# A two-layer model on one core: attention that scores once and transposes in fp32, and a quarter of the scan's input products made on GpSimd

## The reference

```python
x = _layernorm(x + mamba_block(x))      # two selective scans (forward, backward), then a small FFN
x = _layernorm(x + gated_mlp(x))        # silu(x W1) * (x W2), two gelu layers of 512, W3
x = _layernorm(x + attention(x))        # below
x = _layernorm(x + experts(x))          # 8 experts, top 2 by a gate
```

```python
dA = jnp.exp(dt_t[:, :, None] * A)
h = dA * h + (dt_t * u_t)[:, :, None] * B_t[:, None, :]
y = jnp.einsum('bds,bs->bd', h, C_t)
```

```python
scores = jnp.einsum('bqhrd,bkhd->bhrqk', q, k) * scale
scores = jnp.where(causal, scores, jnp.finfo(scores.dtype).min)
probs = jax.nn.softmax(scores, axis=-1)
y = jnp.einsum('bhrqk,bkhd->bqhrd', probs, v)
```

## Time and profile before

| | |
|---|---|
| median of 3 runs | 1955.34 us (1953.61 to 1958.84) |
| profiled execution, its own time | 1948.13 us |
| its span in the trace | 1946.3 us |
| mean granted clock of TensorE | 0.932 of full speed |
| PE busy | 1654.4 us, 85% of the span |
| DVE busy | 1541.2 us, 79% |
| ACT busy | 1114.8 us, 57% |
| POOL busy | 752.7 us, 39% |
| DMA | 309.48 MB, mean 159 GB/s |

### The profile page before, as it was taken

How to read it: one execution, slowest core, us unless ns; L and a number is a source line. 1 busy time by engine, 2 the same in 40 slices (tenths; PEclk the granted TensorE clock), 3 DMA queues, 4 the chain that set the end, 5 groups by cost and what they waited for, 6 DMA issues and landing times.

```text
span 1946.3 us, 26951 instructions
## 1 busy us (share of the span) xinstructions
PE 1654.4 (85%) x8352; PEld 768.0 (39%) x8352; DVE 1541.2 (79%) x2163; ACT 1114.8 (57%) x1553; POOL 752.7 (39%) x601
## 2 busy tenths in 40 slices
PE   3533588889988999889988999889988999889888
PEld 2200134344444435334444435344444435344545
DVE  3999799779995999779995999779996999631514
ACT  3544486467854885567853885567754884433132
POOL 0455454334632454334632454334533454410102
PEclk7655699999999999999999999999999999989999
DMA  7999998667864896668864796667864896500000
GB/s 187 230 244 248 220 242 203 153 156 199 204 153 121 188 216 163 165 143 196 200 156 118 184 218 163 168 147 198 194 156 112 195 219 165 120 0 0 6 1 6
DMA packets 107915, 309.48 MB, mean 159 GB/s; under 512 B 15970, under 2 KB 32244, under 8 KB 107764
## 3 DMA queue, kind: packets, MB, share of 16 engines
q1 hardware_dynamic: 93556, 279.32, 60.9%
q10 hardware_dynamic: 14208, 28.32, 4.5%
HBM read 287.67 MB, written 19.92 MB: 158 GB/s over the span
## 4 chain that ended last, share of the span: by engine, by line
PE 36%; DVE 28%; issue 13%; ACT 13%; DMA 4%; SPq 2%; ACTq 2%; DVEq 1%; POOL 0%; POOLq 0%
PE ps_pair L716 12%; DVE sb_hst L1295 10%; PE ps_pair L813 7%; DMA sb_ring<-spread_dram 4%; PE ps_pair L872 4%; PE ps_pair L801 4%; DVE ps_in L1287 3%; PE ps_pair L892 3%; ACT sb_mix L1129 3%; DVE sb_nmax L1436 2%; ACT sb_ring L971 2%; ACT L940 2%; DVE sb_u L1339 2%; PE ps_pair L816 1%; DVE sb_eh L1504 1%
## 5 line engine op out<-in xcount | busy, mean ns | idle before, releaser
L1567 POOL TENSOR_TENSOR sb_hc<-sb_hst,sb_crep 128x512 f32<-128x512 f32 x512 | 652.8, 1284 | 916.2 <-DVE sb_hst L1295 642.0
L1295 DVE TENSOR_TENSOR_SCAN sb_hst<-sb_ring,ps_in 128x512 f32<-128x512 f32 x512 | 620.0, 1211 | 5.0 <-ACT sb_ring L971 2.5
L971 ACT ACTIVATE sb_ring<-sb_ring,sb_A 128x512 f32<-128x512 f32 x512 | 344.8, 713 | 207.6 <-DMA sb_ring<-spread_dram 116.9
L1287 DVE TENSOR_TENSOR ps_in<-sb_ring,ps_brow 128x512 f32<-128x512 f32 x512 | 354.4, 692 | 29.5 <-DMA sb_ring<-spread_dram 11.5
L940 ACT ACT_TABLE_LOAD x181 | 232.2, 1283 | 46.4 <-issue 39.4
L872 PE MATMUL ps_pair<-sb_mix,sb_ew 128*128 128x512 f32 x512 | 250.0, 624 | 4.6 <-ACT sb_ea L1163 2.2
L651 PE MATMUL ps_y<-sb_hc,sb_const 128*32 128x512 f32 x1024 | 154.2, 678 | 98.8 <-POOL sb_hc L1567 68.7
L813 PE MATMUL ps_pair<-sb_g,sb_h 128*128 128x512 f32 x320 | 168.6, 652 | 15.8 <-DVE sb_dd L1275 5.1
L801 PE MATMUL ps_pair<-sb_h,sb_g 128*128 128x512 f32 (+3 forms) x512 | 165.0, 452 | 13.1 <-DVE sb_nmax L1436 7.8
L872 PEld LDWEIGHTS ps_pair<-sb_mix,sb_ew 128*128 128x128 f32 x512 | 96.6, 198 | 139.1 <-issue 95.3
L892 PEld LDWEIGHTS ps_pair<-sb_ew,sb_eh 128*128 128x128 f32 x1024 | 121.6, 192 | 26.2 <-issue 17.8
(11 more groups left out here) (219 smaller groups left out, 2065.0 us busy)
## 6 DMA issues: line engine op xcount, KB each, us to landing
sb_ring<-spread_dram SPq DMA_DIRECT2D x512, 512.0 KB, 5.9
spread_dram<-sb_dd ACTq DMA_DIRECT2D x32, 512.0 KB, 3.7
sb_brep<-cut_dram ACTq DMA_DIRECT2D x16, 256.0 KB, 4.1
...
```

Source lines behind the costliest of these rows:

```text
L971: act.activation(ring[:, n % RING, 0, :], ring[:, n % RING, 0, :], ACT.Exp, scale=A[d][:, g:g + 1]).then_inc(sem["dA"], 1)
L1287: dve.tensor_tensor(ps_in[n % 2][:], ring[:, n % RING, 1, :], ps_brow[:], ALU.mult).then_inc(sem["dbu"], 1)
L1295: dve.tensor_tensor_scan(hst[:, HST_SLOT[n], :], ring[:, n % RING, 0, :], ps_in[n % 2][:], 0.0, ALU.mult, ALU.add).then_inc(sem["scan"], 1)
L1567: pool.tensor_tensor(hc[:, n % 6, :], hst[:, HST_SLOT[n], :], crep[n // NU][:], ALU.mult).then_inc(sem["hc"], 1)
```

## The change

**Attention.** Scores are made once, with queries on the partitions. A score step is now one bank for one key/value group k, one tile t of 128 queries, and as many of its four heads as fit: four for t = 0, two for t = 1, one for t = 2 and 3 (22 steps, `SCORES`). DVE takes the maximum from the bank (`nmax`), ACT the exponential from the same bank with the negated maximum as bias and with the sum of each row as a second output (`zsum`), one instruction for each head (32). PE transposes the exponentials back in fp32, four blocks of 128x128 for each of 20 `turn` steps; ACT copies the bank into `pT`, and `values` multiplies it with the latent values. The reciprocals of the sums (DVE) are spread over the rows by a product with the identity (`zs`), which ACT copies into `rz` for DVE's `yT`. The second score products, the split, the products with `pick` and `ones`, and 1/sum by exp(-ln) are gone. A sequence's attention has 46 `r` steps in place of 28. Banks are now handed out singly, least recently used first, and `att0` and `att1` hold one each.

**Scans.** Of each four units the last (n % 4 == 3, `POOLED`) has its product with B's rows made by POOL, in place in `ring`, from a copy of B's rows in SBUF (`brep`, now one for each direction). DVE skips `drive` for it, and its `scan` reads both inputs from `ring` in SBUF. These are 16 of a sequence's 64 units.

**Orders.** All strings are new. In DVE's, 88 of its 128 `u` steps stood ahead of the first attention step, with 37 inside the attention; now they are 99 and 25.

```diff
@@ constants and tables
-TILES = ((0, 3), (1, 2))
-ROUNDS = rounds()
+POOLED = [n % 4 == 3 for n in range(UNITS)]
+GROUPS = [(k, t) for k in range(KV) for t in (range(TT) if k == 0 else reversed(range(TT)))]
+SCORES = [(k, t, heads) for k, t in GROUPS for heads in {0: [range(REP)], 1: [range(0, 2), range(2, REP)]}.get(t, [[r] for r in range(REP)])]
+TURNS_P = [(k, t, j) for k, t in GROUPS for j in range(t + 1)]
+PSLOT, PTSLOT = 7, 3
...
 ORDER = dict(
     DVE=(
-        "uxuuxxxurxuxxguuuuuuuuxuxuururxuuxuhrxuuxruuuuuuuuuhrruhuuruhuxuuxruuururuuuuxuuhgruruuuuuuruuuxuuhhuuruuxuuur"
+        "uxuxxxxuuuuguuxuuruuxuuxxuuuruuuuurrhuuuruuxuhuuruuruuruhuururruuururxurhxruguuuuuuhuuuuuurhuuruuuuhuuuuuuuxgu"
...
@@ TensorE
+                def scores(u):
+                    k, t, heads = SCORES[u]
...
+                    for n, r in enumerate(heads):
+                        pe.matmul(o[:, n * w:(n + 1) * w], qT[:, tl, r, :], kz[:, 2 * k + hf, 0:w], start=True, stop=False)
+                        ins = pe.matmul(o[:, n * w + t * P:(n + 1) * w], identb[:], maskb[:], start=False, stop=True)
                     done(ins)
...
+                def turn(x):
+                    k, t, j = TURNS_P[x]
+                    o = claim(f"t{x}")
+                    pe.wait_ge(sem["pexp"], row("pexp", group_scores(k, t)))
+                    for r in range(REP):
+                        slot, at_r = slot_of(k, t, r)
+                        ins = pe.transpose(o[:, r * P:(r + 1) * P], pexp[slot][:, at_r + j * P:at_r + (j + 1) * P], ident)
                     done(ins)
...
+                    elif what == "z":
+                        values(LAST_TURN[i])
+                        o = claim(f"zs{i}")
+                        pe.wait_ge(sem["zr"], row("zr", i + 1))
@@ ScalarE
-                        act.activation(pexp[i % 3], ps_pair[0][:], ACT.Exp).then_inc(sem["pexp"], 1)
...
+                        for n, r in enumerate(heads):
+                            ins = act.activation(pexp[i % PSLOT][:, n * w:(n + 1) * w], bank[tab[f"s{i}"][0][0]][:, n * w:(n + 1) * w], ACT.Exp,
+                                                 bias=nmax[:, k, t, r:r + 1], accum_out=zsum[:, k, t, r:r + 1])
+                        ins.then_inc(sem["pexp"], 1)
+                    elif what == "t":
...
+                        act.activation(pT[:, i % PTSLOT, :], full(f"t{i}")[:], ACT.Copy).then_inc(sem["pt"], 1)
@@ VectorE
+                if POOLED[n]:
+                    return
                 dve.wait_ge(sem["scan"], row("scan", n - 1))
...
             def scan(row, n):
-                dve.wait_ge(sem["dbu"], row("dbu", n + 1))
+                if POOLED[n]:
+                    dve.wait_ge(sem["pbu"], row("pbu", sum(POOLED[:n]) + 1))
+                    dbu = ring[:, n % RING, 1, :]
...
@@ GpSimd
+            def drive(row, n):
+                if n % NU <= 3:
+                    pool.wait_ge(sem["brep"], row("brep", 16 * (n // NU + 1)))
+                pool.wait_ge(sem[f"ring{n % RING}"], row(f"ring{n % RING}", 16 * (n // RING + 1)))
+                pool.tensor_tensor(ring[:, n % RING, 1, :], ring[:, n % RING, 1, :], brep[n // NU][:], ALU.mult
+                                   ).then_inc(sem["pbu"], 1)
+
             def units(at, prev):
                 for n in range(UNITS):
+                    if n + 1 < UNITS and POOLED[n + 1]:
+                        drive(at(0), n + 1)
```

278 lines of the change are left out of this document (123 added, 155 removed).

## The result

The changed kernel takes 1980.4 us (median of 4 runs, 1978.4 to 1982.8); the kernel before takes 1955.4 beside it. The ratio is 1.0126, with a 95% interval of 1.0105 to 1.0147: slower by 25 us, where I had forecast 1865 us, and outside my range. The profiled execution has a span of 1981.0 us and a mean granted clock of 0.908; before it was 1946.3 and 0.932.

A forecast was written before the change was run, and what follows sets the result against it. Passes were taken as bound by DVE outside the attention and by PE in its second half. Five passes -60, second and last sequences -20, flush -15, first sequence +2: -93 from 1948.1, plus 7.2, gives 1862, stated as 1865 us (1825 to 1905).

The forecast's parts named there:

- 56 + 150.5 = 206.5: One pass of the loop: attention plus the stretch outside it, forecast 206.5 us, 12 us less than before.
- The attention at 56: Attention of a pass: engines' work of 44, 41 and 45 us plus a quarter for hand-overs, 56 us (bounds 46 and 78).
- -16 us of about 50: PE's work in each attention: second scores and smaller products go, 80 fp32 transposes come, -16 us of about 50.
- stalls at `yT`: DVE's idle time before `yT` in the attention: forecast to shrink from 15.6 us to about 8 a pass.
- Outside at 150.5: Stretch of a pass outside the attention, bound by DVE: forecast to grow from 140.4 to about 150.5 us.
- The moved units: DVE outside the attention: 11 half units moved there, 5.5 scans and 5.5 products, +10.5 us a pass.
- -8.3 of products: DVE outside the attention: twelve of the products given to POOL lie there and save 8.3 us a pass.
- +6.5 of locks: DVE outside the attention: pooled scans with two SBUF inputs wait for POOL, +6.5 us a pass.
- The third: Rival, chance 0.09: score banks held until ACT is done make PE stand; attention 75 us, pass +7, program 2005 us.
- its 68 us: Attention length in a pass beyond which the bank waits would decide: 56 + 12 = 68 us.
- The second: Rival, chance 0.12: ACT bounds the attention (sums 0.3 each) or PE's clock falls; pass +6 us, program 1915 us.
- The first: Rival, chance 0.12: every pooled scan waits for a full POOL operation; 8 us more a pass, program 1929 us.

The follow-up runs named there:

- unlinked: Changed kernel with exponentials taking a zero bias and waiting for scores alone, DVE's 22 maxima made over a constant tile: 1937.3 us, ratio 0.9935 to the kernel before.
- moved_alone: Kernel before with only its orders changed, 4 scans and 4 products of DVE moved from the attention to in front of it: 1996.4 us, ratio 1.0210.
- no_pool: Changed kernel with all 64 products with B's rows back on DVE, none on POOL: 1984.8 us, ratio 1.0149 to the kernel before.
- pool_load: Kernel before with POOL making 16 products a sequence into an unread tile, DVE still making all 64, scans waiting for POOL: 1979.5 us, ratio 1.0133.
- pool32: Changed kernel with 32 of a sequence's 64 products on POOL in place of 16, orders unchanged: 2104.8 us, ratio 1.0777 to the kernel before.

## Why the prediction was wrong, point by point

**What failed** is the sum for a pass, in both of its terms, as 56 + 150.5 = 206.5; measured in these stretches 63.1 + 160.1 = 223.2.

**The attention at 56.** The forecast priced what each engine has to do (44, 41, 45 us) and added a quarter for hand-overs. PE is busy 51.6 and not 41, and the step that was off is "-16 us of about 50": the 16 were right, the 50 wasn't. The flush of before shows 57.0 of PE in the same attention, so 41 should have stood in place of 34; the flush after has 41.9. Heads and reductions are the other 9.7 us, not 7. The rest is the link over DVE, 5 to 6 us by unlinked; without it 57.5 would have met the 56. A part of all this is the clock, 0.92 or 0.93 in most of these attentions where it was 0.96 before: in unlinked the same work took 2 us more at 0.93 than at 0.97. I had looked at the stalls at `yT` only (forecast 8, measured 4.9) and not at what each maximum adds to a chain that now runs to the end. In the old one DVE's link ended with the sixteenth maximum.

**Outside at 150.5.** The moved units were priced rightly (10.5; measured 10.9, and moved_alone gave 7.2 for 7.6). Wrong was that -8.3 of products, +6.5 of locks and +1.4 of a gate would be the whole rest. no_pool shows 160.2 with no pooled product at all: 2.7 us of the output tokens' norm had been moved out of the attention as well, which I did not list, 1.3 is the gate, 1.1 is in the dt chain, and 4.5 is more idle time. The locks of the 13 pooled scans there cost 2 us and not 6.5, but the dt chain and the norm are drawn out by 3 more, which I had at nothing. Before, DVE was busy 130.8 of 140.2, after 143.2 of 160.1; I added no idle time to it, and there the step failed. By these cuts, at the first maximum, a pass has 141.8 outside before, and not the 140.4 that I started from. PE stands too: its reductions have 5.4 us of idle in front of them in the changed kernel (0.0 before), waiting for POOL's `hc`.

```profile
L677 PE MATMUL ps_y<-sb_hc,sb_const 128*32 128x512 f32 x112 | 15.8, 636 | 5.4 <-POOL sb_hc L1566 5.3
```

**The products on POOL.** DVE's busy time a pass came out as forecast (185.8 against 185), the locks of the scans smaller (0.14 against 0.45 a scan). The error was to take DVE's work for the length of the stretch. Of the 8.6 us outside, 5.5 went into slower instructions, and the 3.1 of work that stayed saved came back as idle time (+3.0).

**What was right.** PE's attention: -15.1 us in the flush, where it stands alone (57.00 to 41.88, at a clock of 0.94 where it had been 1.00), forecast -16. The flush 53.4 (51). The first sequence +1.2 us to its 64th scan (+2). ACT's 157.6 a pass (160), though each sum cost 0.19 and not 0.1. The idle time before `yT`, 4.9 (under 10). The second and last sequence missed as the passes did: the last one's attention went from 68.9 to 52.2 and the stretch ahead of it from 134.4 to 158.8.

**The rivals.** The third came nearest, since it put the loss on hand-overs. It put them on the banks, though, which no run took apart, and the link that unlinked cut goes over the maximum; PE's longest waits are for POOL's `hc` (104 us in all), not for `pt` (36) or `pexp` (23). The attention never reached its 68 us; the kernel is slower at 63, since the bar it had to clear was set by the 150.5. The second is true in part: the clock in the attention is 0.92 in place of 0.96, and ACT's sums are worth 1.5 us each attention. None of its signs came: ACT is busy 157.6 of a pass and not over 175, and the clock stays over 0.9. The first asked for scans of over 2.2 us, and they take 1.35; POOL's load did cost in other kernels (pool_load +26, pool32 +124), in this one nothing that could be told.

**What stays open.** How much of the 160 us is the fault of the written orders, and how much no order could save: four of the five orders that I rewrote are 70 us and more slower than those they were made from, and for three of them a row above shows a wait that is new, so none tells how good the order of the changed kernel is for it. That units in the old attention were nearly free rests on one order, moved_alone. And the part of the clock: no run changed it alone. An estimate from unlinked (some 2.3 us of an attention between 0.97 and 0.93) gives 1.5 us for each of the first six attentions of the changed kernel and 3 for the flush's, some 12 us in all.
